# Local attention of a perceiver block: the softmax's division moved behind the product with the values

## What is computed

```
def _L0_attn_ref(x, ...):                  # B=4, N=256, D=256, H=16 heads of dh=16, W=64
    Q = (x @ q_w.T + q_b).reshape(B, N, H, dh)
    K = (x @ k_w.T + k_b).reshape(B, N, H, dh)
    V = (x @ v_w.T + v_b).reshape(B, N, H, dh)
    ...                                    # each block of 64 rows sees its own and the previous 64 keys
    scores = jnp.einsum('bnqhd,bnkhd->bnhqk', Qb, Kw) / math.sqrt(dh)
    scores = jnp.where(mask[None, :, None, :, :], scores, -jnp.inf)
    wts = jax.nn.softmax(scores, axis=-1)
    out = jnp.einsum('bnhqk,bnkhd->bnqhd', wts, Vw).reshape(B, N, D)
    return out @ o_w.T + o_b

x = x + _L0_xattn_ref(_layernorm(x), ctx_1024, ...)
x = x + _L0_attn_ref(_layernorm(x), ...)
x = x + _L0_ffn_ref(_layernorm(x), ...)    # router, two of eight experts a row
```

## Time and profile before

| | us |
|---|---|
| median of 3 runs (lowest, highest) | 589.95 (589.87, 590.14) |
| the profiled execution, its own time | 590.69 |
| its span, first to last instruction | 589.0 |
| busy in the span: TensorE | 567.4 (96%) |
| VectorE | 409.1 (69%) |
| ScalarE | 338.8 (58%) |
| GpSimd | 248.5 (42%) |
| mean granted clock of TensorE, 1 is full speed | 0.994 |

### The profile page before, as it was taken

How to read it: one execution, slowest core, us unless ns; L and a number is a source line. 1 busy time by engine, 2 the same in 40 slices (tenths; PEclk the granted TensorE clock), 3 DMA queues, 4 the chain that set the end, 5 groups by cost and what they waited for, 6 DMA issues and landing times.

```text
span 589.0 us, 9978 instructions
## 1 busy us (share of the span) xinstructions
PE 567.4 (96%) x3765; PEld 485.4 (82%) x3765; DVE 409.1 (69%) x682; ACT 338.8 (58%) x577; POOL 248.5 (42%) x258
## 2 busy tenths in 40 slices
PE   7999999999999999989999989999999999999995
PEld 5889988997899889966676767888888888888884
DVE  3957685668566855498889678776767676767661
ACT  5768535854584346447766726747465655656450
POOL 4176256625751664244545431334242424233312
PEclk9999999999999999999999899999999999999998
DMA  8994292029202000000005948999999999999642
GB/s 278 420 414 192 93 411 69 1 99 404 69 3 68 4 1 2 1 0 2 2 2 189 393 179 308 329 350 317 353 323 355 339 343 349 326 349 320 211 142 89
DMA packets 25167, 119.27 MB, mean 203 GB/s; under 512 B 2640, under 2 KB 8912, under 8 KB 14096
## 3 DMA queue, kind: packets, MB, share of 16 engines
q1 hardware_dynamic: 20752, 112.48, 50.8%
q0 software_dynamic: 4368, 6.16, 5.1%
HBM read 113.52 MB, written 6.42 MB: 204 GB/s over the span
## 4 chain that ended last, share of the span: by engine, by line
PE 80%; DVE 8%; DMA 4%; issue 3%; ACT 2%; POOL 2%; POOLq 0%; SPq 0%; DVEq 0%; ACTq 0%
PE psum L1672 20%; PE psum L1449 15%; PE psum L1403 13%; PE psum L1689 12%; PE psum L1309 11%; PE psum L1365 3%; DVE head_max L974 2%; DVE region_a L979 1%; DMA region_w<-ctx_cols_dram 1%; PE psum L1547 1%; POOL wide_low L565 1%; DMA region_w<-sums_by_token,tokens 1%; DMA sums_by_token<-region_w,tokens 1%; PE psum L1331 1%; PE psum L1411 1%
## 5 line engine op out<-in xcount | busy, mean ns | idle before, releaser
L680 ACT ACTIVATE wide_high<-region_a 128x1024 fp32r<-128x1024 f32 (+1 forms) x104 | 104.9, 1009 | 97.8 <-PE psum L1672 94.0
L1139 DVE TENSOR_TENSOR wide_low<-region_a,wide_high 128x1024 fp32r<-128x1024 f32 x92 | 112.1, 1221 | 58.1 <-ACT wide_high L680 58.1
L1689 PE MATMUL psum<-region_a,region_w 128*128 128x256 f32 x368 | 83.3, 379 | 0.0
L1064 DVE TENSOR_TENSOR turned_low<-psum,turned_high 128x512 fp32r<-128x512 f32 x64 | 43.8, 690 | 55.3 <-ACT turned_high L680 55.2
L1449 PE MATMUL psum<-turned_high,wide_low 128*128 128x256 f32 x256 | 78.5, 307 | 0.8 <-DVE turned_low L1064 0.2
L1672 PE MATMUL psum<-wide_low,turned_high 128*128 128x512 f32 x184 | 78.2, 425 | 0.3 <-DVE turned_high L1241 0.2
L1689 PEld LDWEIGHTS psum<-region_a,region_w 128*128 128x128 f32 x368 | 69.7, 190 | 10.0
L1672 PE MATMUL psum<-wide_high,turned_low 128*128 128x512 f32 x184 | 72.4, 394 | 0.0
L1449 PE MATMUL psum<-turned_high,wide_high 128*128 128x256 f32 x256 | 72.2, 282 | 0.0
L1449 PE MATMUL psum<-turned_low,wide_high 128*128 128x256 f32 x256 | 72.1, 282 | 0.0
L1672 PE MATMUL psum<-wide_high,turned_high 128*128 128x512 f32 x184 | 72.1, 392 | 0.0
(11 more groups left out here) (225 smaller groups left out, 1160.6 us busy)
## 6 DMA issues: line engine op xcount, KB each, us to landing
region_a<-up_weights_dram SPq DMA_DIRECT2D x23, 2048.0 KB, 9.7
region_a<-down_weights_dram SPq DMA_DIRECT2D x23, 1024.0 KB, 7.1
region_w<-ctx_cols_dram SPq DMA_DIRECT2D x32, 512.0 KB, 9.4
region_a<-ctx_dram SPq DMA_DIRECT2D x16, 1024.0 KB, 12.3
third_weights<-third_weights_dram SPq DMA_DIRECT2D x1, 1035.0 KB, 26.8
residual<-x_dram SPq DMA_DIRECT2D x4, 256.0 KB, 7.9
sums_by_token<-residual SPq DMA_DIRECT2D x2, 512.0 KB, 9.5
normed_rows<-region_s SPq DMA_DIRECT2D x4, 256.0 KB, 6.4
```

The source lines that it names most:

```text
L680: return nc.scalar.activation(dst, src, ACT.Copy)
L1064: nc.vector.tensor_tensor(pT_lo[:, g % 2], probs_bank(g).rearrange("p (k n) -> p k n", k=PAIR), pT_hi[:, g % 2].bitcast(F32), ALU.subtract ...
L1139: nc.vector.tensor_tensor(w_lo[:, k % RING], group_of(k), w_hi[:, k % RING].bitcast(F32), ALU.subtract).then_inc(low_ready, 1)
L1689: last = nc.tensor.matmul(to[:, 0:D], hidT[n][:, ic * P:(ic + 1) * P], rows, start=ic == 0, stop=ic == IC - 1)
```

## The change

Five things are changed.

1. GpSimd no longer multiplies by the reciprocal. It adds the two halves of each head's 128 exponentials (512 numbers a row for the unit) and then the two quarters of that (256 numbers a row); `halved` and `quartered` follow. VectorE sums the 256.
2. The turns take the exponentials as they are and wait for `local_exp`. In TensorE's iteration the scores of unit n+3 now stand ahead of the turns of unit n.
3. VectorE's reciprocal writes 128 numbers a row, each head's repeated 16 times, into one of two buffers (`inv_rows`). Behind the PV product of unit n TensorE multiplies this by the identity into the second part of bank 6, which turns it to the layout of the output, and `localpv_done` now follows this product. The reciprocal of unit n waits until the product of unit n-2 has read the buffer.
4. ScalarE copies the turned reciprocal to SBUF (`inv_copied`), and VectorE multiplies bank 6 by it into `headsT` (`local_out`), so `heads_ready` now comes from VectorE.
5. The value bias goes into the output bias: in batch 0, behind the ninth PV group, two matmuls multiply it by the output weights into bank 2, and VectorE adds that to the bias rows.

```
@@ GpSimd
             for n, (b, u) in enumerate(WORK):
-                pool.wait_ge(inv_ready, n + 1)
-                nc.gpsimd.tensor_tensor(local[u], local[u], over_keys(hinv[:, u, :]), ALU.mult).then_inc(normed, 1)
+                pool.wait_ge(local_exp, n + 1)
+                if n > 0:
+                    pool.wait_ge(quartered, n)
+                nc.gpsimd.tensor_tensor(half_sums, local[u][:, :, 0:WIN], local[u][:, :, WIN:P], ALU.add).then_inc(halved, 1)
+                pool.wait_ge(halved, n + 1)
+                if n > 1:
+                    pool.wait_ge(row_sum, n - 1)
+                nc.gpsimd.tensor_tensor(quarter_sums[n % 2], half_sums[:, :, 0:QUAD], half_sums[:, :, QUAD:WIN], ALU.add).then_inc(quartered, 1)
@@ ScalarE
-            def local_out(n):
-                b, u = WORK[n]
-                t, hc = UNITS[u]
+            def local_inverse(n):
                 act.wait_ge(localpv_done, n + 1)
-                last = nc.scalar.activation(headsT[:, hc, b * NTOK + t * P:b * NTOK + (t + 1) * P], bank[6][:, 0:P], ACT.Identity,
-                                            bias=vbc[:, hc:hc + 1])
+                last = copy(inv_wide, bank[6][:, P:2 * P])
                 if n == GATE_MEAN:
                     last = copy(gate_mean[:, :], mean_sum)
-                last.then_inc(heads_ready, 1)
+                last.then_inc(inv_copied, 1)
@@ VectorE
                 if n >= len(UNITS):
                     dve.wait_ge(local_turned, GROUP0[n - len(UNITS) + 1])
+                    dve.wait_ge(halved, n - len(UNITS) + 1)
             def local_sum(n):
                 b, u = WORK[n]
-                dve.wait_ge(local_exp, n + 1)
-                nc.vector.tensor_reduce(hsum[:, u, :], local[u], axis=X_AXIS, op=ALU.add).then_inc(row_sum, 1)
+                dve.wait_ge(quartered, n + 1)
+                nc.vector.tensor_reduce(hsum[:, u, :], quarter_sums[n % 2], axis=X_AXIS, op=ALU.add).then_inc(row_sum, 1)
                 dve.wait_ge(row_sum, n + 1)
-                nc.vector.reciprocal(hinv[:, u, :], hsum[:, u, :]).then_inc(inv_ready, 1)
+                if n > 1:
+                    dve.wait_ge(localpv_done, n - 1)
+                nc.vector.reciprocal(inv_rows[n % 2].rearrange("p (h a) -> p h a", h=HPC),
+                                     hsum[:, u, :].rearrange("p (h a) -> p h a", a=1).broadcast_to([P, HPC, DH])).then_inc(inv_ready, 1)
+
+            def local_out(n):
+                b, u = WORK[n]
+                t, hc = UNITS[u]
+                dve.wait_ge(inv_copied, n + 1)
+                nc.vector.tensor_tensor(headsT[:, hc, b * NTOK + t * P:b * NTOK + (t + 1) * P], bank[6][:, 0:P], inv_wide, ALU.mult).then_inc(heads_ready, 1)
@@ VectorE, the loop over the units and the row groups
                 if n + LOOK < len(WORK):
                     local_max(n + LOOK)
+                if 0 < n < len(WORK) - 1:
+                    local_out(n - 1)
             output(0)
             output(1)
+            local_out(len(WORK) - 2)
             inverse_root(0)
             output(2)
+            local_out(len(WORK) - 1)
@@ TensorE
                     for g in range(PAIRS):
                         weigh(g)
+                        if b == 0 and g == V_BIAS:
+                            ...
+                            for c in range(DC):
+                                last = nc.tensor.matmul(bank[2][:, 0:D], vbc[:, c:c + 1].broadcast_to([P, P]), owT[:, c, :], start=c == 0, stop=c == DC - 1)
+                            last.then_inc(v_bias_done, 1)
-                last.then_inc(localpv_done, 1)
+                pe.wait_ge(inv_ready, n + 1)
+                nc.tensor.matmul(bank[6][:, P:2 * P], inv_rows[n % 2], ident[:, :], start=True, stop=True).then_inc(localpv_done, 1)
             for n in range(len(WORK)):
-                pe.wait_ge(normed, n + 1)
-                local_turn(n, 0)
-                local_turn(n, 1)
                 if n + LOOK < len(WORK):
                     ...
                     local_score(n + LOOK)
+                pe.wait_ge(local_exp, n + 1)
+                local_turn(n, 0)
+                local_turn(n, 1)
```

## The result

The changed kernel takes 630.55 us (median of 4 runs, 627.24 to 635.39). The kernel before took 590.05 beside it (589.87 to 590.71). The ratio is 1.069, 95% interval 1.066 to 1.072: 6.9% slower. 628 was predicted, with a range of 616 to 639.

A forecast was written before the change was run, and what follows sets the result against it. TensorE and VectorE were taken to alternate as the bound in local attention. 29.0 (laps) + 7.7 (tail) + 0.9 (batch 0) = 37.6; 590.7 + 37.6 - 0.7 = 627.6, given as 628, range 616 to 639.

The forecast's parts named there:

- What bounds the kernel: Local attention before the change: TensorE and VectorE take turns at being last, mean lap 4.45 us, bare VectorE lap 4.00.
- Rival D: Local attention: the reciprocal's buffer wait doesn't bind, laps 4.32 or 4.69 us; 601 us, chance 0.06.
- Part 1, the sum: VectorE's reduction falls from 1.21 to 0.42 us; GpSimd's additions, about 2.0 us per unit, stay hidden.
- the ring: Local attention laps in series: subtraction, TensorE's part but the fill, reciprocal, maximum, next subtraction; 6.87 us against 4.45.
- Part 2, the reciprocal: VectorE's reciprocal grows from 8 to 128 elements: 0.95 to 1.25 us, or about 0.33 if like a copy.
- Part 3, the ring: The reciprocal's wait for the identity product of unit n-2 lengthens 12 local attention laps: +29.0 us.
- rival B: Local attention: the ring plus two to six laps at half clock, 2.9 us more each; 634 to 645 us, chance 0.15.
- Part 4, the tail: From unit 15's subtraction (S) to the routing's first maximum, output additions and products come later: +7.7 us on 17.6.
- Part 5, batch 0: Two float32 matmuls 128x256 for the value bias on TensorE's full path in batch 0: +0.9 us.
- Moving the scores ahead of the turns gains nothing in this ring; both are in it: TensorE's new order in local attention: no gain, since scores and turns both lie in the serial lap.
- The signs: Profile marks of right or wrong: L1559 wait some 2.3 us a unit, subtractions 6.9 apart, reciprocal 0.95 to 1.25, additions 10 late.

The follow-up runs named there:

- all repairs: The changed kernel with a third buffer, GpSimd's two extra steps later, the tail reordered, and the reciprocal over 8 elements with a 16-fold copy: 593.41 us, ratio 1.0048.
- the run on the order: The changed kernel with a third buffer, and VectorE's first output additions and ScalarE's roots and inverse copies earlier in the tail: 596.00 us, ratio 1.008.

## Why the prediction was right, point by point

**What bounds the kernel.** That TensorE and VectorE alternate was right, the reason was half right. "A bare lap of VectorE ... is ... 4.00 us" named one loop where two have the same length: VectorE's own, and the loop over the score banks, which is from the prediction's terms 1.38 + 0.52 + 0.65 + 0.13 + 1.32 = 4.00. In the kernel before they can't be told apart; the run with all repairs separated them. It moved nothing in the forecast, but it made the expectation of the last run on the change (all repairs) 2.2 us too low. Rival D's laps were wrong for another reason: 4.32 and 4.69 were given, some 3.97 and 4.82 were measured with a third buffer. In the bare lap the reciprocal was given as 1.13 and takes 0.87 to the maximum, and the output product was given as 0.28 and adds 0.20; in the full lap the identity product was given as 0.24 and adds 0.33, the turns take 0.14 more and the fill 0.11 less.

**Part 1, the sum.** Reduction 0.42 given, 0.41 measured. GpSimd's halves and quarters were given as 1.29 and 0.65 to 1.0; in the order of time they last 1.27 and 0.73. The two laps in which it is late were costed at nothing under the cover of the ring, and so it came: in one the sum waits 2.37 us for GpSimd, the reciprocal behind it only 0.43 for TensorE, and the lap is 6.81; in the other the sum does not wait. Without the cover the waits are 2.37 and 1.67, as the prediction's "about 2 us each", and moving the steps gives 2.25 us of laps back.

**Part 2, the reciprocal.** 1.1 was taken, between slopes that gave 0.95 and 1.25; it is 0.953. That is the slope of the rows for two and eight elements (6.2 ns an element), carried on to 128 without a bend.
**Part 3, the ring.** Right in mechanism, and shown by three runs: the third buffer opens the loop, and taking the reciprocal's 0.43 or the turns' 1.03 out of it shortens the lap by that much. The size was 6.87 given, 6.81 in a clean lap. That it fits so closely is partly luck, as errors of 0.33 and 0.36 us cancel. Two terms were low, the turns (0.88 given, 1.03 between the scores and the PV product) and the identity product with the way to VectorE (0.42 given, 0.60); two were high, the reciprocal with its end (1.13 given, 0.87) and the subtraction to the masks (1.38 given, 1.28). The 12 laps came to +31.6 in place of +29.0. Without its own error of 0.06 a lap (0.7 in all) the forecast would be 3.3 short: 2.9 us are the two laps with half clock in them (8.09 + 8.41 - 2 x 6.81), which was rival B, and 0.35 is the gate's mean in the lap of 7.16, which the list of the ring's steps left out. The low clock did not come at rival B's full price of 2.9 a lap but at 1.3 and 1.6, since the low clock covers the turns and the products behind them in the one, and the scores and the turns in the other, not all of TensorE's part. So the execution shown is the forecast's mechanism with a small part of rival B's, and the spread of 627 to 635 us goes with the clock. That the clock is its cause is not shown.

**Part 4, the tail.** +7.7 given, +6.6 measured. The first addition was put at S+9.95 and stands at S+9.5, the output product of unit 14 at S+16.45 (S+15.8), the last addition at S+21.5 (S+20.7). Little of this is the ring: with a third buffer the tail is still 23.66 us, 0.6 less. The mechanism, ScalarE's inverse copy behind the high part and VectorE's additions behind output products, was tested by the run on the order, which gave 4.55 us of tail back. The last 1.5 were not taken apart.

**Part 5, batch 0.** +0.9 given, 0.86 in the chain, 1.0 as the median of the run alone.

**"Moving the scores ahead of the turns gains nothing in this ring; both are in it".** The time was forecast for the new order, and there both are in it. But that the move changes nothing was not right: in the old order the turns stand outside the ring, and the run with the product ahead of the turns puts their price inside it at 1.03 us a lap. By itself, on the kernel before, it gains 1.1 us. Of the two parts that were run alone, this and the value bias, it is the one that gains; the others were not run alone.

**The sum and rival D.** The terms gave 37.6. The spans differ by 39.2 (31.6 for 29.0 in the laps, 6.6 for 7.7 in the tail, 1.3 for 0.9 ahead of unit 3, and 0.4 less behind the tail, for which nothing was given), the times of the two executions by 39.6 (630.25 against 590.69). So a ring that was put too low and a tail that was put too high cancel in part. Rival D, the same kernel without the ring, was given as 601 and was measured at 601.58, but its parts were less exact than that: laps +3.0 in place of +2.5, tail +6.1 in place of +7.7. The profiled execution of that kernel was the fastest of its four, 599.85. The remaining 1.7 us of the median stand in executions whose profile isn't shown, so what they are stays open.

**The signs.** The reciprocal's wait for L1559 is the largest new one, as forecast, but 2.91 us in a clean lap and not 2.3; the forecast's own terms give 2.6. The subtractions stand 6.8 us apart with and without a fill (6.9 given), the reciprocal reads 0.953, the first addition stands 9.5 us behind the last subtraction (10 given), and the clock between 270 and 350 us is 0.96, above the 0.9 that would have spoken for B.

## What to carry to other kernels

A new wait for a buffer is priced by what its release stands behind: write down the whole loop, from the waiting instruction over every engine back to it, and compare that with the lap of today. Here the engine that waits stood ahead of the work that releases it, 6.8 us in a lap of 4.45, and one more buffer of 128 columns opened the loop. Before a step is made cheaper, look whether its lap is bound by that engine or by another loop of the same length; a wait that moves to the next instruction (0.43 us for 0.43 us saved) is how the second loop shows.

## What the runs showed of the hardware

- The reciprocal of 128 elements lies on the slope of the small ones, 6.2 ns an element: 166 ns for two, 203 for eight, 953 for 128. Eight reciprocals and a 16-fold copy in SBUF take 0.20 + 0.23 us, less than half of it.
- Eight turns of 128x128 take 0.87 us to the next line behind a projection and ahead of the masks, 0.93 behind score products and ahead of a product of 128 rows, and 1.02 to 1.03 behind score products and ahead of the PV product.
- TensorE's granted clock fell to 0.50 for some 3 us shortly behind gaps of 3.21 and 2.78 us, in two laps of twelve, and not behind two gaps of 2.69 us. TensorE was busy 54.75 of 80 us in that stage. The four executions of the changed kernel differ by 8 us, and the slower ones have the lower mean clock. The four of the kernel before beside them differ by 0.8; in a set of 17 of them (589.02 to 593.22, mean clocks of 0.990 to 0.994) one lay over 3 us above the median without a lower clock.
- GpSimd's float32 addition takes 1.27 us for 512 elements a partition and 0.73 for 256.
